# A routed two-block layer: the split h stays on chip, x is updated in place, one register load a step, and another VectorE order

## What is computed

```
e   = min(clip(token, 0, 24999) // 6250, 3)
h   = layernorm(x)
g   = silu(h @ ctx[e].T);  u = h @ ctx[e].T
x   = x + tanh(g_xattn) * ((g * u) @ ctx[e])
h2  = layernorm(x)
w   = weights of the top 2 of softmax(h2 @ Wr + br), made to sum to 1
out = x + tanh(g_ffn) * sum_e w[e] * (relu(h2 @ Wd[e] + bd[e]) @ Wu[e] + bu[e])
```

## Time and profile before

| | |
|---|---|
| median of three runs | 214.99 us (211.97 to 216.06) |
| the profiled execution | 212.24 us, its span 209.6 us |
| mean granted TensorE clock | 0.945 of full speed |
| TensorE busy | 168.0 us, 80% of the span |
| VectorE busy | 133.9 us, 64% |
| GpSimd busy | 123.7 us, 59% |
| ScalarE busy | 119.3 us, 57% |
| DMA | 22.00 MB, mean 105 GB/s |

### The profile page before, as it was taken

How to read it: one execution, slowest core, us unless ns; L and a number is a source line. 1 busy time by engine, 2 the same in 40 slices (tenths; PEclk the granted TensorE clock), 3 DMA queues, 4 the chain that set the end, 5 groups by cost and what they waited for, 6 DMA issues and landing times.

```text
span 209.6 us, 5618 instructions
## 1 busy us (share of the span) xinstructions
PE 168.0 (80%) x1570; PEld 117.2 (56%) x1570; DVE 133.9 (64%) x385; ACT 119.3 (57%) x237; POOL 123.7 (59%) x313
## 2 busy tenths in 40 slices
PE   1756877699959957997989889899799999575680
PEld 1644765577636636765657567476576675244220
DVE  4949686954675856757476675766766765784431
ACT  2686598694558457465484754846846745351100
POOL 5478843634554256585766767556466465567561
PEclk9999999789999997999999999999999999999555
DMA  5937668633234533726628344284563334121022
GB/s 151 390 95 222 205 160 139 87 92 87 52 86 95 90 65 90 150 30 124 78 77 112 90 104 87 69 150 76 79 153 59 96 100 91 59 56 52 0 100 100
DMA packets 44157, 22.00 MB, mean 105 GB/s; under 512 B 39753, under 2 KB 39881, under 8 KB 44129
## 3 DMA queue, kind: packets, MB, share of 16 engines
q1 hardware_dynamic: 41568, 13.26, 32.5%
q0 software_dynamic: 2560, 8.39, 13.0%
HBM read 9.06 MB, written 4.19 MB: 63 GB/s over the span
## 4 chain that ended last, share of the span: by engine, by line
POOL 24%; issue 22%; DVE 17%; ACT 13%; DVEq 11%; PE 7%; DMA 3%; ACTq 1%; POOLq 1%; SPq 0%
DVEq L1259 6%; DVEq L1258 3%; POOL rs L502 3%; POOL half_first L553 3%; ACT h L943 3%; POOL rs L492 2%; POOL xs L474 2%; ACT h_parts L951 2%; DVE h_parts L1251 2%; DMA hT<-h_parts 2%; POOL hot_slot L467 2%; POOL mrs L503 2%; DVE xs L1266 2%; ACT h L908 2%; DVE weighted L1327 2%
## 5 line engine op out<-in xcount | busy, mean ns | idle before, releaser
L688 PE MATMUL ps_a<-hT,w_hi 128*128 128x128 f16 x304 | 65.4, 226 | 4.8 <-DMA hT<-h_parts 4.2
L689 PE MATMUL ps_a<-hT,w_hi 128*128 128x128 f16 x304 | 65.1, 225 | 0.0
L690 PE MATMUL ps_a<-hT,w_lo 128*128 128x128 f16 x304 | 65.1, 225 | 0.0
L689 PEld LDWEIGHTS ps_a<-hT,w_hi 128*128 x304 | 30.7, 101 | 19.9 <-issue 1.7
L688 PEld LDWEIGHTS ps_a<-hT,w_hi 128*128 x304 | 30.6, 101 | 11.5 <-issue 8.4
L702 PE MATMUL ps_y<-w_hi,pT_hi 128*128 x76 | 29.5, 388 | 2.6 <-DVE pT_lo L1284 2.4
L690 PEld LDWEIGHTS ps_a<-hT,w_lo 128*128 x304 | 30.6, 101 | 0.2
L892 ACT ACTIVATE dev_sq<-xs,sum 128x512 f32<-128x512 f32 x14 | 10.1, 723 | 33.9 <-DVE xs L1266 33.9
L702 PE MATMUL ps_y<-w_lo,pT_hi 128*128 x76 | 29.3, 386 | 0.0
L702 PE MATMUL ps_y<-w_hi,pT_lo 128*128 x76 | 29.1, 383 | 0.0
L1266 DVE SCALAR_TENSOR_TENSOR xs<-ps_y,y_t,xs 128x512 f32 x19 | 14.3, 750 | 20.1 <-issue 20.0
(11 more groups left out here) (242 smaller groups left out, 414.2 us busy)
## 6 DMA issues: line engine op xcount, KB each, us to landing
w_nat<-in_ctx_dram SPq DMA_DIRECT2D x4, 1024.0 KB, 8.1
hT<-h_parts SPq DMA_TRANSPOSE x18, 3.9
xs<-in_x_dram,rows_of POOLq DMA_INDIRECT x16, 4.1
wd_nat<-in_L_ffn_Wd_dram SPq DMA_DIRECT2D x8, 32.0 KB
wu_nat<-in_L_ffn_Wu_dram SPq DMA_DIRECT2D x1, 256.0 KB
out_dram<-xs,rows_of POOLq DMA_INDIRECT x16, 3.2
h2T<-h_parts SPq DMA_TRANSPOSE x14, 3.1
b_in<-in_L_ffn_bd_dram SPq DMA_DIRECT2D x1, 64.0 KB
```

What stands on the lines that cost most here:

```text
L688: mm(ps[:, c, :], hi, hi_h[:, kc, :], start=(kc == 0), stop=False)
L689: mm(ps[:, c, :], hi, lo_h[:, kc, :], start=False, stop=False)
L690: last = mm(ps[:, c, :], lo, hi_h[:, kc, :], start=False, stop=(kc == KC - 1))
```

## The change

1. `h_parts` becomes one buffer of 16 tiles (`[P, T, 2, D]`). ScalarE and VectorE normalise and split each tile once, at its own index, without a register: 16 times, not 19, and tile 0 too. normalise1, h_high and h_low drop out of steps 14 to 16, and h_high no longer waits for a transpose.
2. SP loads the pair's tile number into a register before each `transpose_h` and takes the source from `h_parts` by it; before transpose_h(1) it waits for `s_places`. ScalarE's register loads and its wait for `s_places` are gone.
3. `xs` has 16 tiles, and add_y, squares, normalise2, add_low_rank and the scatter all work on it in place. The four GpSimd operations for the source number are gone, and with them VectorE's second register load.
4. VectorE's step begins product(i-1), add_y(i-3), then the one register load, find_tile(i-1), then statistics1 and the rest. In the tail product(18) comes before add_y(16), and one load before pT_low(18).

```diff
--- before.py
+++ after.py
@@ -115,10 +115,6 @@
         expert_i = sb("expert_i", [P, NP], i32)
         pair_tile = sb("pair_tile", [P, NP])
         pair_tile_i = sb("pair_tile_i", [P, NP], i32)
-        new_tile = sb("new_tile", [P, NP])
-        again = sb("again", [P, NP])
-        source_f = sb("source_f", [P, NP])
-        source_i = sb("source_i", [P, NP], i32)
 
 
         w_nat = sb("w_nat", [P, E, KC, D])
@@ -178,8 +174,7 @@
         out_coef = sb("out_coef", [P, 1])
 
 
-        xs = sb("xs", [P, 2 * T, D])
-        x1 = xs[:, T:2 * T, :]
+        xs = sb("xs", [P, T, D])
         st1 = sb("st1", [P, 6])
         mv1 = sb("mv1", [P, 2])
         st2 = sb("st2", [P, 6])
@@ -192,7 +187,7 @@
         mrs = sb("mrs", [P, 2, T])
         neg_half = sb("neg_half", [P, 1])
         h = sb("h", [P, D])
-        h_parts = [sb(f"h_parts{b}", [P, 2, D], fp16) for b in range(2)]
+        h_parts = sb("h_parts", [P, T, 2, D], fp16)
         hT = [sb(f"hT{b}", [P, 2, KC, P], fp16) for b in range(3)]
         silu = sb("silu", [P, KC, P])
         prod = [sb(f"prod{b}", [P, KC, P]) for b in range(2)]
@@ -391,11 +386,12 @@
 
             def transpose_h(k):
 
-                sp.wait_ge(h_lo_done, k)
+                tile = sp.value_load(pair_tile_i[0:1, col(k)], min_val=0, max_val=T - 1)
+                sp.wait_ge(h_lo_done, min(k + 1, T))
                 if k > 2:
                     sp.wait_ge(a_done, k - 2)
                 sp.dma_start_transpose(hT[k % 3][:, :, :, :].rearrange("p s c q -> p (s c) q"),
-                                       h_parts[k % 2][:, :, :].rearrange("p s d -> p (s d)"))\
+                                       h_parts[:, col(tile), :, :].rearrange("p o s d -> p (o s d)"))\
                   .then_inc(s_hT[k - 1], 16)
 
             def transpose_h2(k):
@@ -419,6 +415,7 @@
                     sp.dma_start(gates_in[:, 0:1], g_xattn.rearrange("(a n) -> a n", a=1).to_broadcast([P, 1])).then_inc(s_gates_in, 16)
                     sp.dma_start(gates_in[:, 1:2], g_ffn.rearrange("(a n) -> a n", a=1).to_broadcast([P, 1])).then_inc(s_gates_in, 16)
                 if t == AHEAD - 1:
+                    sp.wait_ge(s_places, 1)
                     transpose_h(1)
                     sp.dma_start(b_in[:, 0:ER], bd.rearrange("(a e) r -> a (e r)", a=1).to_broadcast([P, ER])).then_inc(s_small, 16)
                     sp.dma_start(b_in[:, ER:HC], br.rearrange("(a e) -> a e", a=1).to_broadcast([P, EF])).then_inc(s_small, 16)
@@ -460,7 +457,6 @@
                 g.memset(w_rep[b][:, :, :, :], 0.0)
             g.memset(b_rows[:, :], 0.0)
             g.memset(ones16[:, :], 1.0)
-            g.memset(new_tile[:, 0:1], 1.0)
             g.memset(sq_parts[:, :], 0.0).then_inc(s_const, 1)
             pool.wait_ge(s_in_tile, 1)
             for c in range(DVE_HOT, C):
@@ -523,13 +519,7 @@
 
                 then(g.tensor_tensor(pair_tile[:, :], pair_no[:, :], expert_f[:, :], ALU.subtract))
                 then(g.tensor_scalar(pair_tile[:, :], pair_tile[:, :], float(T - 1), None, ALU.min))
-                g.tensor_copy(pair_tile_i[:, :], pair_tile[:, :])
-
-                then(g.tensor_tensor(new_tile[:, 1:NP], pair_tile[:, 1:NP], pair_tile[:, 0:NP - 1],
-                                     ALU.subtract))
-                then(g.tensor_scalar(again[:, :], new_tile[:, :], -float(T), float(T), ALU.mult, ALU.add))
-                then(g.tensor_tensor(source_f[:, :], again[:, :], pair_tile[:, :], ALU.add))
-                g.tensor_copy(source_i[:, :], source_f[:, :]).then_inc(s_places, 1)
+                g.tensor_copy(pair_tile_i[:, :], pair_tile[:, :]).then_inc(s_places, 1)
 
             def y_factors(n, p0, p1):
 
@@ -572,7 +562,7 @@
                 g.indirect_dma_start(
                     out=out_rows[:, :],
                     out_offset=bass.IndirectOffsetOnAxis(ap=rows_of[:, k:k + 1], axis=0),
-                    in_=x1[:, k, :], in_offset=None,
+                    in_=xs[:, k, :], in_offset=None,
                 ).then_inc(s_scatter, 16)
 
             for i in range(-3, NP):
@@ -889,7 +879,7 @@
 
                 act.wait_ge(x1_done, k + 1 + LATE)
                 wait_last(act, ssq2_done, k)
-                a(dev_sq[:, :], flat(x1[:, col(k), :]), ACT.Square, bias=sum2[:, col(k)], scale=-float(D),
+                a(dev_sq[:, :], flat(xs[:, col(k), :]), ACT.Square, bias=sum2[:, col(k)], scale=-float(D),
                   accum_out=ssq2[:, col(k)]).then_inc(ssq2_done, 1)
 
             def weights_high(k):
@@ -905,7 +895,7 @@
                     wait_last(act, h2_lo_done, k)
                 else:
                     act.wait_ge(h2T_done, k - BY_DMA)
-                a(h2[:, :], flat(x1[:, col(k), :]), ACT.Identity, bias=mrs[:, 1, col(k)],
+                a(h2[:, :], flat(xs[:, col(k), :]), ACT.Identity, bias=mrs[:, 1, col(k)],
                   scale=rs[:, 1, col(k)]).then_inc(normed2, 1)
 
             def h2_high(k):
@@ -927,28 +917,19 @@
                 wait_last_but(1, act, w8_done, k)
                 a(half_tanh[k % 2][:, :], gap[k % 2][:, :], ACT.Tanh, scale=half_inv[:, :]).then_inc(tanh_done, 1)
 
-            tiles = [0]
-
-            def find_tile(k):
-
-                tiles.append(act.value_load(pair_tile_i[0:1, col(k)], min_val=0, max_val=T - 1))
-
             def normalise1(k):
 
-                tile = tiles[k]
-                act.wait_ge(rstd1, min(k + 1, T))
+                act.wait_ge(rstd1, k + 1)
                 if k == 1:
                     act.wait_ge(hT_done, 1)
-                wait_last_but(1, act, h_lo_done, k)
-                a(h[:, :], flat(xs[:, col(tile), :]), ACT.Identity,
-                  bias=mrs[:, 0, col(tile)], scale=rs[:, 0, col(tile)]).then_inc(normed1, 1)
+                wait_last(act, h_lo_done, k)
+                a(h[:, :], xs[:, k, :], ACT.Identity, bias=mrs[:, 0, k:k + 1],
+                  scale=rs[:, 0, k:k + 1]).then_inc(normed1, 1)
 
             def h_high(k):
 
                 act.wait_ge(normed1, k + 1)
-                if k > 2:
-                    act.wait_ge(s_hT[k - 3], 16)
-                a(h_parts[k % 2][:, 0, :], h[:, :], ACT.Copy).then_inc(h_hi_done, 1)
+                a(h_parts[:, k, 0, :], h[:, :], ACT.Copy).then_inc(h_hi_done, 1)
 
             def step(i, meanwhile=None):
 
@@ -957,8 +938,6 @@
                 if some(ON_ACT, -3 - LATE, i):
                     squares2(i - 3 - LATE)
                 product_high(i - 1)
-                if some(NP, 2, i):
-                    find_tile(i + 2)
                 if meanwhile:
                     meanwhile()
                 if some(T, -5 - LATE, i):
@@ -968,7 +947,7 @@
                     h2_high(i - 3 - LATE)
                 if some(T, -4 - LATE, i):
                     half_tanh_of(i - 4 - LATE)
-                if some(NP, 2, i):
+                if some(T, 2, i):
                     normalise1(i + 2)
                     h_high(i + 2)
 
@@ -982,11 +961,9 @@
             square_sums(2, range(0, 2))
             normalise1(0)
             square_sums(2, range(2, KC))
-            act.wait_ge(s_places, 1)
             act.wait_ge(hT_done, 1)
             a(hT[0][:, 0, :, :], ps_hT[:, :, :], ACT.Copy).then_inc(hT_hi_done, 1)
-            find_tile(1)
-            find_tile(2)
+            h_high(0)
             normalise1(1)
             h_high(1)
             high_parts(1)
@@ -1247,24 +1224,23 @@
 
             def h_low(k):
 
-                dve.wait_ge(h_hi_done, k)
-                v.tensor_tensor(h_parts[k % 2][:, 1, :], h[:, :], h_parts[k % 2][:, 0, :],
+                dve.wait_ge(h_hi_done, k + 1)
+                v.tensor_tensor(h_parts[:, k, 1, :], h[:, :], h_parts[:, k, 0, :],
                                 ALU.subtract).then_inc(h_lo_done, 1)
 
-            places = []
-
-            def place(k):
-
-                return (dve.value_load(pair_tile_i[0:1, col(k)], min_val=0, max_val=T - 1),
-                        dve.value_load(source_i[0:1, col(k)], min_val=0, max_val=2 * T - 1))
+            tiles = []
+
+            def find_tile(k):
+
+                tiles.append(dve.value_load(pair_tile_i[0:1, col(k)], min_val=0, max_val=T - 1))
 
             def add_y(k):
 
-                tile, source = places[k]
+                tile = tiles[k]
                 dve.wait_ge(y_done, k + 1)
                 wait_last(dve, x1_done, k)
-                v.scalar_tensor_tensor(flat(x1[:, col(tile), :]), ps_y[k % 2][:, :], y_t[:, col(k)],
-                                       flat(xs[:, col(source), :]), ALU.mult, ALU.add,
+                v.scalar_tensor_tensor(flat(xs[:, col(tile), :]), ps_y[k % 2][:, :], y_t[:, col(k)],
+                                       flat(xs[:, col(tile), :]), ALU.mult, ALU.add,
                                        accum_out=sum2[:, col(tile)]).then_inc(x1_done, 1)
 
             def statistics2(k):
@@ -1272,7 +1248,7 @@
                 n = k - ON_ACT
                 dve.wait_ge(x1_done, k + 1 + LATE)
```

(17 more changed lines are left out.)

## The result

Four runs of the changed kernel gave 197.09 to 199.60 us, median 197.76; the kernel before on the same chip, 213.48 (209.71 to 216.06). The ratio is 0.939 [0.926, 0.953]: 6.1% faster, where 203.0 us against 214.99, 5.6%, had been forecast. On the scale of that 214.99 it is 201.9 us. The profiled spans, 209.6 and 195.8 us, differ by 13.8 us, where the sum had 9.9. The direction came out, and the sum was 3.9 us short. That the ratio came so near is in part luck: 9.9 us are 4.7% of the profiled execution, and the forecast's 5.6% has 2.1 us more in it, since it counted 203.0 from near the low time of that execution and set it against the higher median.

The account below looks back on a forecast made before the run. A circle of waits through VectorE, ScalarE and GpSimd was taken to set the pace until about step 13, then TensorE. 7.0 + 1.4 + 1.5 = 9.9 us off 212.24 gave 202.3, set at 203.0 towards the median; range 199 to 210.

Parts of the forecast that it names:

- The circle: Steady loop add_y, squares, GpSimd's rstds and choice, w, h_low, next add_y: 8.65 us, to become 8.0; 3.6 us gained.
- The gap behind add_y: VectorE's one load, now ahead of statistics, pT_low and best_two: a 0.6 us gap, hidden, costed at 0.
- given back on GpSimd: Rival: later pT_low lies over GpSimd's rstd and returns 0.5 us a step; gain only 5.4 us, chance 0.17.
- The front: Start of the kernel: four GpSimd operations leave, other work comes in; between -0.4 and +0.4 us, taken as 0.
- the 3.4: Steps 3 to 6, where the chain runs through product: add_y at 77.94 moves 3.4 us earlier, range 1.5 to 5.
- The last stage: Last five steps, without second normalising: TensorE's 7.47 us a step saves 2.4 us, less 0.4 and 0.6, leaving 1.4.
- the 0.4 for add_low_rank's later place: Deduction from the last five steps: TensorE's restart in step 13 waits for add_low_rank, 0.4 us later in the new order.
- The 0.6 for a late landing: Deduction from the last five steps: an h2T transpose can land after 4.9 us instead of 3.1; 0.6 us off.
- The tail: After the last steps: pT_low of the last pair starts some 1.5 us earlier, everything after keeps its length; -1.5 us.
- SP's loads: 18 register loads ahead of SP's hT transposes, 0.30 to 0.83 us each, covered by its wait for h_low; costed at nothing.
- The rival on the slower side: Add_y behind product behind silu forms a loop; transposes landing after 8.5 us make 217.4 or 218 us, chance 0.06.
- No change: Rival: transposes' landing paces steps 3 to 8 and the last five; 3.0 us off, 212 us, chance 0.12.

Follow-up runs that it names:

- the single load: Changed kernel with VectorE's old order (add_y before product) and its one register load at the step's end: 197.44 us, ratio 0.924.
- add_y first: Changed kernel with add_y ahead of product again, the register load still behind both: 196.47 us, ratio 0.919.
- the choice first: Changed kernel with GpSimd's choice moved ahead of the next tile's rstd: 197.98 us, ratio 0.930.
- two loads: Changed kernel with a second VectorE register load, its value unused, right behind the first: 199.45 us, ratio 0.933.
- the order alone: Kernel before with only VectorE's new order, both register loads behind add_y: 202.73 us, ratio 0.948.
- the memory scheme alone: Changed kernel with VectorE's old order and two register loads at the step's end, the second unused: 206.91 us, ratio 0.969.
- three loads: Changed kernel with three register loads on SP ahead of each hT transpose, two of them unused: 200.72 us, ratio 0.940.
- the two traces of the changed kernel: The first profile and that of a repeat without any edit, which took 197.93 us, ratio 0.932 against the kernel before.

## Why the prediction was right, and where its sum was short

**The circle and its term: right.** Steps 7 to 13 gave 52.15 - 48.09 = 4.06 us where 3.6 stood; 8.0 us a step was forecast, 7.98 came. (By its own terms the sum makes 8.65 - 0.58 = 8.07; product begins 0.60 us after h_low and not 0.67, so add_y stands at 1.26 and not 1.34.) TensorE's hT wait in step 5 is gone (near 1 us was said), and the h2T wait ends at 75.60 (near 77). One sign failed: ps_o's wait in the steady steps was to stay, and 0.81 became 0.21 in one step and no visible wait in the others. And pT_low(18)'s "issue" wait is gone: it now waits 1.40 us for ScalarE's high part.

**What made it: only half right.** I credited the order. The experiments say that the order and the single load each do it alone: with the memory scheme in place, the span is 204.9 with neither, 195.2 with the single load, 196.4 with the order, 195.8 with both. They aren't terms to be added, and mine came out, by luck rather than by insight, because I had counted the gap once, under the order. The rest of the 13.8 us, from 209.6 to 204.9, is the memory scheme's without either: 1.30 of it ahead of the add_y of step 3 and 1.49 in steps 13 to 18.

**The gap behind add_y: wrong, harmlessly.** I put 0.6 us ahead of the statistics, "half the old 1.24". The load costs 0.00 there in the steady steps, and a second one too. In these traces a load's price isn't its duration; it goes by what VectorE has queued when its sequencer reaches it. Of the rival *given back on GpSimd* nothing is seen: rs took 0.57. It stood one step further on, though: with add_y first, or the choice first, pT_low begins just ahead of rs and takes 0.50 us back. rs is at 1.07 when pT_low began 0.05 us before it, and at 0.57 when it had begun 0.19 us before pT_low, whose 0.69 wasn't lengthened either. The Trainium skill (SBUF — State Buffer, Who interferes with whom) says that the order of issue decides which of the two is blocked. GpSimd's side agrees with it: 1.07 us when it began second, 0.57 when it began first. A blocked VectorE operation isn't seen in these rows.

**The front: the step that failed.** It was taken as 0 (±0.4), and 0.92 us came: pair 4's h_low starts at 48.33 and not at 49.25. (The add_y of step 3 comes 1.49 us earlier; the other 0.57 is its shorter distance from h_low, which the 3.4 already held.) Put back, the four GpSimd operations cost 0.84 us at that add_y and at that h_low, and 1.59 at the add_y of step 7; how much of the further 0.75 is theirs stays open, for in that trace SP's small DMAs ran longer too (hT(2) at 38.48). What I had set against them, two ScalarE and VectorE operations and SP's load for pair 2, takes nothing back: hT(2) was issued 0.98 us after the last small DMA, at 37.02, and wasn't waited for. Front and steps 3 to 7 together are 1.49 + 3.10 = 4.59 us where 3.4 stood: 1.2 more, 0.92 of it the front. I had priced the operations about right, at some 1.1 us for 0.84, and set something off against them that didn't stand on the same path.

**The last stage: mis-sized, and put down to the wrong part.** Between the `ps_o` matmuls of steps 13 and 18 lie 162.92 - 125.99 = 36.93 us, 7.39 a step, against 39.78: 2.85 where 1.4 stood. TensorE's pace was 0.4 us better than the 7.47 us of the sum. Of the 0.4 for add_low_rank's later place, 0.28 shows ahead of this stretch: from add_y to `ps_o` step 13 takes 4.55 us, not 4.27, though the row at 125.99 has no wait for VectorE. The 0.6 for a late landing didn't come in this trace; with two loads it did (1.03 us at 130.93), and with the order alone (1.11 us at 134.04), so here it was luck. By add_y, steps 13 to 18 gave 3.63: the order alone gives 2.61, with the second normalising left in, and the memory scheme alone 1.49. So "no second normalising" wasn't needed for TensorE's pace.

**The tail: 1.5 forecast, 2.6 measured** (from `ps_o` of step 18 to the end, 35.46 to 32.88). Of this 1.97 lie ahead of the last add_y, and 0.61 behind it, where the matmuls are the same and the clock is higher (0.77, not 0.69).

**SP's loads: 0 was right for one, by less than I said.** 0.98 us stands ahead of hT(2), and with three loads product(2) came 1.2 us later. My cover, SP's wait for h_low, holds neither there nor in the steady steps, where hT is issued 0.34 us later behind h_low than before: the load, which starts at 104.0 and takes 0.81 us, ends later than h_low does. What makes it free is that TensorE needs hT over a step later, which I had named only for steps 14 and on.

**The rival on the slower side** asked for transposes landing after 8.5 us. With the source address from a register they land after 3.1, 3.6 and 5.9 us (least, median, most), against 3.1, 3.9 and 5.9. *No change* wanted transposes that pace the steps whatever the circle does; its two waits, 2.45 and 3.41 us, fell to none and 1.91.

The differences, 1.2 (front and steps 3 to 7), 0.5 (7 to 13), 1.2 (the 1.45 of the last stage less the 0.28 in step 13) and 1.1 (tail), make the 3.9 us. The ratio's 201.9 lies within 199 to 210; the median itself, 197.76, lies 1.2 us under it. The low end allowed for 1.6 us more in steps 3 to 7 and 0.6 for no late landing, 2.2 in all (202.3 - 2.2 is 200.1, so 199 was already a microsecond under its own terms), where 3.9 came. The ratio falls inside since 214.99 was a high median of the kernel before: it had 213.48 with the fourth run, and 212.36 to 213.15 beside the experiments.

## What to carry to other kernels

When a register load stands in a chain, look at what its engine has queued when the sequencer reaches it: behind two operations of 0.7 us even two loads cost the chain nothing, in front of the operation that is waited for one costs 0.47 and two 1.10 us. If two edits close the same gap, test each alone before adding their terms, and take the cheaper. Compare stages and not spans: here the stretch behind the last add_y took 24.05 to 26.84 us over the kernels and differed by 0.6 between two traces of the same one, as much as many single edits were worth. The clock early on mattered less: over the first 48 us its mean was 0.93 with two loads and 0.86 and 0.82 in the two traces of the changed kernel, and the first add_y came at 49.55, 49.60 and 49.60.

## What the runs showed of the hardware

- A register load on VectorE runs ahead of operations that stand before it in the program: it began at 96.4 us, product and add_y at 96.84 and 97.50. In the kernels before and after, loads took 0.30 to 0.83 us. In the steady steps those that began within 0.25 us of h_low's start took 0.69 to 0.83; but a busy VectorE alone doesn't make a load long: with two loads, the second began at 97.4, with product under way, and took 0.30.
- On SP, between DMAs, a load holds the queue for 0.98 us, and three for 2.06.
- A VectorE operation with two SBUF inputs that began just ahead stretched four different GpSimd operations: rs from 0.57 to between 1.02 and 1.11, arg8f from 0.19 to 0.57, half_sum from 0.20 to 0.75, half_first from 0.33 to 0.83. VectorE's own 0.67 to 0.69 us didn't change. An rs that began 0.18 or 0.19 us first kept its 0.57.
- A DMA transpose whose source address comes from a register lands as fast as one with a fixed address: 3.1, 3.6 and 5.9 us against 3.1, 3.9 and 5.9.
- The granted clock stood at its lower level (1.2 of 2.4 GHz) in the last one to three of the 40 slices of every kernel, where TensorE was busy for about half the time (13.06 of 25.62 us), and the tail took 24.05 to 26.84 us. In the changed kernel it also stood there in the fourth and fifth slice (15 to 24 us); in the kernel before it didn't.
